# GpSimd zeroes the masked exponentials of layer two, in place of a mask added to the scores by TensorE

## The reference, cut to what matters

```python
scores = jnp.einsum('bhsl,bhtl->bhst', q_lat, c) * (1.0 / np.sqrt(L))
mask = jnp.tril(jnp.ones((Sx, Sx), dtype=bool))
scores = jnp.where(mask, scores, -jnp.inf)
w = jax.nn.softmax(scores, axis=-1)
oh = jnp.einsum('bhst,bhtd->bhsd', w, v)
```

## Time and profile before

| | us |
|---|---|
| median of 3 runs | 2285.42 (2282.18 to 2289.64) |
| the profiled execution | 2285.18 |
| its span, first to last instruction | 2283.5 |
| TensorE busy in the span | 1969.4 (86%) |
| VectorE, ScalarE, GpSimd busy | 1104.0, 864.6, 738.3 |
| mean granted TensorE clock | 0.907 of full |

### The profile page before, as it was taken

The page is one execution under the profiler, slowest core; times in us unless marked ns, Lnnn a source line. Parts: engine busy times, 40 slices in busy tenths (PEclk is TensorE's granted clock), DMA queues, the critical chain, the costliest instruction groups (busy, mean ns, idle before and its releaser), DMA issues.

```text
span 2283.5 us, 47852 instructions
## 1 busy us (share of the span) xinstructions
PE 1969.4 (86%) x16112; PEld 1298.2 (57%) x16112; DVE 1104.0 (48%) x2561; ACT 864.6 (38%) x1624; POOL 738.3 (32%) x796
## 2 busy tenths in 40 slices
PE   3464899998989999898898999998998989998978
PEld 1232475665647565565746566564756556574747
DVE  3544455462645445373645537273554536363422
ACT  2341433434343343435343343534343343533322
POOL 2000233333424333333423333342433333342425
PEclk7566899989989899999999899998999999999979
DMA  4612321313232231413231141313232141322130
GB/s 111 146 42 60 62 50 44 84 36 86 45 67 54 57 66 37 95 36 82 50 71 41 42 94 37 89 42 67 56 68 53 37 93 37 79 57 63 30 70 5
DMA packets 320767, 139.28 MB, mean 61 GB/s; under 512 B 225040, under 2 KB 306000, under 8 KB 320592
## 3 DMA queue, kind: packets, MB, share of 16 engines
q1 hardware_dynamic: 305232, 86.24, 16.0%
q0 software_dynamic: 15360, 50.34, 10.7%
HBM read 102.12 MB, written 29.88 MB: 58 GB/s over the span
## 4 chain that ended last, share of the span: by engine, by line
issue 48%; POOL 18%; PE 14%; DMA 8%; DVE 5%; SPq 3%; ACT 3%; POOLq 1%; DVEq 0%; ACTq 0%
POOL h2l L681 7%; POOL gs L675 6%; DMA cb<-comb_d 6%; PE s3r L1287 3%; POOL cb L669 3%; PE s2acc L1284 2%; POOL h1p L626 1%; SPq L539 1%; PE s2r L1287 1%; PE s2r L1495 1%; DVE th L1172 1%; SPq L500 1%; POOL va L649 1%; PE s2r L1497 1%; PE s1acc L1390 1%
## 5 line engine op out<-in xcount | busy, mean ns | idle before, releaser
L675 POOL TENSOR_TENSOR gs<-gs,cb 128x512 f32<-128x512 f32 x192 | 243.4, 1268 | 471.9 <-DVE gs L1177 285.1
L681 POOL TENSOR_TENSOR h2l<-th,h2h 128x512 f16<-128x512 f32 (+1 forms) x224 | 246.8, 1102 | 377.6 <-ACT h2h L871 377.6
L871 ACT CAST h2h<-th 128x512 f16<-128x512 f32 (+1 forms) x224 | 131.4, 587 | 499.4 <-DVE th L1172 482.1
L1287 PE MATMUL s3r<-xe,xg 128*128 128x256 f16 x2304 | 284.3, 273 | 21.1 <-issue 21.1
L1287 PE MATMUL s3r<-xe,xu 128*128 128x256 f16 x2304 | 285.0, 274 | 9.4 <-DVE th L1172 9.4
L1284 PE MATMUL s2acc<-xd,h2h 128*128 128x256 f16 x1536 | 280.3, 285 | 3.8 <-POOL h2l L681 3.5
L1177 DVE SCALAR_TENSOR_TENSOR gs<-th,s3r 128x512 f32<-128x512 f32 (+1 forms) x224 | 145.1, 648 | 266.8 <-ACT th L875 266.8
L1287 PEld LDWEIGHTS s3r<-xe,xg 128*128 128x128 f16 x2304 | 223.1, 98 | 57.5 <-issue 31.8
L1287 PEld LDWEIGHTS s3r<-xe,xu 128*128 128x128 f16 x2304 | 223.8, 98 | 42.0 <-DVE th L1172 10.0
L1172 DVE TENSOR_TENSOR th<-s3r,gs 128x512 f32<-128x512 f32 x192 | 132.6, 691 | 235.7 <-POOL gs L675 193.4
L875 ACT ACTIVATE th<-s3r 128x512 f32<-128x512 f32 (+1 forms) x224 | 126.6, 565 | 302.8 <-PE s3r L1287 302.1
(11 more groups left out here) (268 smaller groups left out, 3225.3 us busy)
## 6 DMA issues: line engine op xcount, KB each, us to landing
cb<-comb_d POOLq DMA_DIRECT2D x192, 256.0 KB, 8.0
part_d<-part SPq DMA_DIRECT2D x32, 512.0 KB, 3.3
va<-v_d SPq DMA_DIRECT2D x512, 8.0 KB
land<-part_d SPq DMA_DIRECT2D x96, 64.0 KB, 2.6
part<-part_d SPq DMA_DIRECT2D x96, 64.0 KB, 2.6
qst<-part_d SPq DMA_DIRECT2D x96, 64.0 KB, 2.3
kst<-part_d SPq DMA_DIRECT2D x96, 64.0 KB, 2.3
x<-in_L_attn_x SPq DMA_DIRECT2D x16, 256.0 KB, 2.8
```

Of the source, the lines that this page charges most:

```text
L675: g.tensor_tensor(gc2[:, p % 2, :], gs2[:, p % 2, :], cb2[:, 2 * p:2 * p + 2, :].rearrange("p a s -> p (a s)"), ALU.mult).then_inc(sem("gc ...
L681: g.tensor_tensor(h2l[0:m, n % 2, 0:w], th2[0:m, n % 2, 0:w], h2h[0:m, n % 2, 0:w], ALU.subtract).then_inc(sem("h2l_made"), 1)
L871: s.copy(h2h[0:m, n % 2, 0:w], th2[0:m, n % 2, 0:w]).then_inc(sem("h2h_made"), 1)
L1287: ins = nc.tensor.matmul(bk, lhs[i][k], rhs[j][k], start=first, stop=last)
```

## The change

The matmul of the mask (L1541) goes; the last score matmul of each head signals the bank full. GpSimd gets eight steps of its own, one per K step: it waits for both heads' exponentials and writes zeros above the diagonal into the two diagonal blocks of both slots, in one `affine_select` of 128 x 512 numbers, in place. `weigh` waits for that and no longer for the exponentials. `TURNS` is another order of the same steps.

```diff
-TURNS = [int(c) for c in ("022202121100221001210201212202102220122212101210101010131002"
-                         "021301001010310133113010004103041000040303043030033440303330"
-                         "33313")]
+TURNS = [int(c) for c in ("022221002112021010102201212202102212022212101021101013102120"
+                         "003010101101013011330310000401410300040033343300030403033343"
+                         "33130")]
@@ gp2
-            for n in range(2 * HG + 8):
+            for n in range(HG + 5):
+                yield
+            for n in range(0, H, 2):
+                for i in (n, n + 1):
+                    gp.wait_ge(*emptied2(it, U2["k_rows", i]))
+                    carry(gp, "gp_waited")
+                x = p2[:, n % PSLOT:n % PSLOT + 2, :].rearrange("p s (c n) -> p s c n", n=P)[:, :, 0:3:2, :]
+                g.affine_select(out=x, in_=x, pattern=[[0, 2], [0, 2], [1, P]], compare_op=ALU.is_ge, fill=0.0, base=0,
+                                channel_multiplier=-1).then_inc(sem("p2_masked"), 1)
+                yield
+            for n in range(3):
                 yield
@@ pe2, weigh
-                pe.wait_ge(*emptied2(it, U2["k_rows", QUAD * q + QUAD - 1]))
+                pe.wait_ge(*event("p2_masked", it, 2 * q + 2))
@@ pe2, K steps
-                        mm(ring2[u % 2][:, at:at + S - P * j], head(kst2, h, QK1)[:, P * j:P * j + P],
-                           head(qst2, h, QK1)[:, P * j:S], start=j == 0, stop=False, skip_group_check=True)
-                for u, h in pair:
-                    mm(two(ring2[u % 2])[:, :, 0:P], identb[:, :], maskk1[:, :].unsqueeze(1).to_broadcast([P, T, P]),
-                       start=False, stop=True, skip_group_check=True).then_inc(fills2(u), 1)
+                        ins = mm(ring2[u % 2][:, at:at + S - P * j], head(kst2, h, QK1)[:, P * j:P * j + P],
+                           head(qst2, h, QK1)[:, P * j:S], start=j == 0, stop=j == T - 1, skip_group_check=True)
+                        if j == T - 1:
+                            ins.then_inc(fills2(u), 1)
```

## The result

| | us |
|---|---|
| before, median of 4 runs beside those of after | 2283.8 (2280.15 to 2289.64) |
| after, median of 4 runs | 2354.33 (2338.53 to 2364.75) |
| ratio | 1.0300, 95% interval 1.0238 to 1.0363 |
| the profiled execution of after, and its span | 2355.37, 2353.7 |
| its mean granted TensorE clock | 0.894 of full (before 0.907) |

The change costs 71 us. The direction was forecast, the size was not: 2305 was predicted, and 2344 was the upper end of the range.

A forecast was written before the change was run, and what follows sets the result against it. The prediction took PE, 86% busy, as the engine to save on, its saving turned into waits. Per pass +3.1 and -1.7 give +1.4 us, +20 over 14 passes: 2285.2 + 20 = 2305 us, range 2256 to 2344.

The forecast's parts named there:

- The masks' saving: K steps: PE's time saved by dropping the masks all turns into waits for ScalarE and VectorE; weigh 3 1.7 later.
- The part ahead of T: Before the older experts' last `down` ends: two layer-one row scores move behind it, so this part loses 1.7 us.
- the sum: Per pass, +3.1 us behind the older experts' last `down`, -1.7 ahead of it: +1.4, over 14 passes +20 us.
- its sign: PE's waits at `up 3` and `k 12`: together over 3 us a pass; wrong if 2.6 or under, or K stretch shorter.
- the last stretch: Last K stretch, counted apart: masks go (5 us), four select waits of about 1 us come; put at nothing.
- one stretch of 3.4 us: PE between `k 12` and `turned 1`: half-rate clock expected after idles of 3 and 2, 1.7 us lost.
- The select: GpSimd's zeroing instruction: 0.95 us each, between 0.66 and 1.36; it hides at 0.95 and decides from about 1.3.
- The masks' worth: PE's mask matmuls in the K steps: removing them gains at most 41 us over 16 passes, at least nothing.
- A: Rival, faster: PE stays the bound, waits do not form; whole gain 2244 us, half 2265; chance 0.28.
- B: Rival, no change: K-stretch saving and the later weight transfer cancel; 2279 to 2292 us; chance 0.14.
- C: The forecast itself, slower: 2292 to 2325 us; chance 0.38.
- D: Rival, slower still: select takes 1.36 us, or PE's idle brings a further half-rate stretch; with both 2340 us; chance 0.20.

The follow-up runs named there:

- e17: The kernel after with the first 56 steps of a pass (the front) in the order of before; 2308.07 us, 1.0079 against before.
- e2: The kernel before, mask added by PE and no select, with the changed kernel's order of steps; 2361.78 us, 1.0321 against before.
- e3: The kernel after with the mask matmuls left in as well as GpSimd's zeroing; 2364.41 us, 1.0303 against before.
- e5: The kernel after with the old order of steps behind weigh 3 (the tail); 2396.09 us, 1.0459 against before.
- e9: The kernel after with the twelve weight transfers issued by SP instead of GpSimd, at the same step; 2305.67 us, 1.0092 against before.
- e14: GpSimd zeroing and weight transfers issued by SP, new order for the first 56 steps, old order behind; 2283.54 us, 0.9986 against before.
- e18: The kernel before, masks by matmul, with only the first 56 steps of a pass in the new order; 2301.25 us, 1.0076 against before.
- e1: The kernel after, with GpSimd's zeroing, but the steps in the old order; 2396.14 us, 1.0473 against before.
- e7: The kernel before with GpSimd's twelve weight transfers issued early, ahead of `xbe`; 2323.6 us, 1.016 against before.
- e8: GpSimd's zeroing in the old order, with GpSimd's twelve weight transfers issued early, ahead of `xbe`; 2345.64 us, 1.026 against before.
- e6: The kernel after with GpSimd's twelve weight transfers issued early, ahead of `xbe`; 2356.15 us, 1.0301 against before.
- e4: The kernel before without the second pass's mask, neither matmul nor select, in the old order; 2286.51 us, 0.9996 against before.
- e12: The kernel before without the second pass's mask, neither matmul nor select, old order, weight transfers issued by SP; 2253.04 us, 0.983 against before.
- e10: The kernel before, old masks and old order, with the twelve weight transfers issued by SP; 2251.7 us, 0.9823 against before.

## Why the prediction was wrong in size

**What held.** In the pass shown: weigh 0 at T + 8.3 (8.9 forecast), weigh 3 at T + 22.8 (22.7), `weights 0` at T + 23.6 (23.2), the product of `gate 2` at T + 43.0 (42.4), `up 3` at T + 45.0 (44.5), `k 12` at T + 49.8 (49.3), `turned 1` at T + 59.4 (58.0). The masks' saving is turned into waits for ScalarE: the weighs' wait for `p` went from 21.5 us to 33.9, and it is ScalarE and not the select that they wait for, as the second select was done 0.9 us before weigh 0. The part ahead of T is 2.0 us shorter (1.7 forecast). With the old front, as the prediction in effect assumed it, the sum comes out: e17's periods are 1.53 us longer than before (1.4 forecast), its T to weigh 3 1.75 (1.7), and it takes 2308 us where 2305 was forecast.

**What agreed for other reasons.** The prediction named as its sign PE's waits at `up 3` and `k 12`, together over 3 us a pass, and called itself wrong if they stay at 2.6 or under. They are 0.55 and 1.39 us in the pass shown, where idles of 3 and 2 were forecast, and 2.5 us a pass over the 14 passes, no more than before's 2.8 at `k 12` alone. By its own sign it is wrong there. `up 3` does start when the weights' chain lets it, but PE reaches it at T + 44.5 and not at T + 41.5: in the new tail it waits on the way for the next sequence's x (L960, 17.5 us in all) and for `part` (L991, 16.4), where before has 0.2 us a pass behind ScalarE and 2.6 us in all. The walk had these two at nothing. That e17 meets the sum is thus partly luck: 2.5 us a pass too much at two waits, 2.0 too little at two others, 3.3 us in all that the last stretch takes more, and 1.0 by which the first T comes sooner.

**The step that failed** is "The sum": "+3.1 behind T and -1.7 ahead of it". It took the order as changed only around the K steps. The diff also permutes the 56 steps in front (21 of their digits differ), which I neither spelled out nor walked through, and so entered as zero. On top of the new K steps and tail they cost 46 us (after against e17), mainly in three places of the table: 1.9 us a pass before the row scores (36.55 against 34.66), 1.1 from T to weigh 3, and 8.4 us at the two ends. The forecast was 49 short.

**The clock.** I gave the half rate one stretch of 3.4 us behind the idles at `up 3` and `k 12`. From weigh 3 to `turned 1` there is less of it than before, 1.5 us a pass against 2.9; it came elsewhere. Among seven kernels with the new front (after, e2, e3, e5, e9, e14, e18), 4 to 9 passes of 14 have over 3 us at half rate before the row scores, and at most one in any with the old front. (e9's profile is of its fastest execution, 2288.96 us.) Over 10 us at half rate from T to weigh 3 is found in 17 of 70 passes of the five that have the new front and the new K steps (after, e2, e3, e5, e9), in 2 of 28 of the two that have the new front and the old K steps (e14, e18), and in none with the old front, except where PE waits long within the stretch: three passes of e1, those with 12 to 14 us at weigh 3, and passes of e7 and e8, where the early weights make it wait for the row maxima (so does e6, left out of the count).

Fewer masks are not the reason (e3; and e4, without any, has 447 us at half rate in its span, before 427). From T to T the half-rate time is 13.4 us a pass in before, 16.9 in after, 10.5 in e17 and 12.6 in e18. Between e17 and after PE's idle time is nearly the same, 16.4 and 16.5 us, so the 2.7 us of the period lie in the 6.4 us more at half rate; between before and e18 idle time grows from 11.9 to 13.4 and the clock adds nothing. The front thus costs waits by itself, and clock on top of the new K steps. The tie between front and clock is shown as one that goes together; how the order in front brings the clock down in some passes and not in others stays open, and each kernel has one profile only.

**The single prices.** The select takes 0.64 us; I took 0.95 with 0.66 as the lower end, so it lies just under it. The Trainium skill's 769 ns ("GPSIMD Engine Reference", Elementwise side-by-side cycle accounting) was nearer than my value and still above the measured 637. It mattered little, since the select hides in the new order: of all the weighs of after one is put down to it, with 1.3 us. The masks' worth I bounded by 0 and 41 us; the runs say 0, to within 6 us (e4 against before; e12 against e10 agrees). The 28 us that the Trainium skill's gap of 109 ns gave ("TensorE: Matmul & The Clock Gate", Back-to-back issue gap) is PE time, and no run shows it as time of the kernel. The last stretch I put at nothing: it took 6.5 us more, 3.3 of them still in e17 (98.7 us from the last T to the end). The weights are awaited there with no tail to hide them: PE's wait for `th` of `up 3` is 13.7 us, where before has 9.2.

**The rivals.** A fell: weigh 3 isn't at T + 20.96 or before, and e4 shows that even with no select PE's saving does not reach the end. B fell by the time alone. C has the direction and the times of the landmarks, D the sign of the remainder: there was more half rate, but not behind the idle where D placed it, and its select was shorter, not longer.

**What the change is worth.** Without the new front 21 to 25 of its 71 us are left, the price of the later weights with the K steps and tail that make room for them (e17). The new front costs 46 on top of these and 14 by itself (e18), so over 30 us come only where both stand together, and no single part owns them; with SP's weights the front costs 44 on top of them and 32 by itself. Its aim, to relieve TensorE of the masks, was worth nothing here, for it relieved an engine that waits at the weighs anyway. What was to be gained lay in the issue of the weights in GpSimd's queue: moved to SP, with the old masks and the old order, the kernel takes 2251.7 us, 1.8% less than before (e10).

## What to carry to other kernels
When a diff holds a reordered list, decode and walk the whole of it, also where none of the changed operations stand; here the permutation of 56 steps cost 14 us by itself and 46 on top of the rest, which alone cost 21. Before an engine is relieved of work, leave the work out altogether and time that: it bounds the gain, and here the bound was zero. An instruction added to a queue is priced by what stands ahead of it there (in e1 weigh 3 waits 102 us for selects behind the twelve issues on GpSimd, while all selects of after take 81), and bulk transfers belong in a queue where nothing short waits behind them.

## What the hardware did that I had not expected
The twelve issues on GpSimd are sometimes cut in two by a gap without any wait, 7.82 us in e1's row above. It is regular: in all twelve kernels in which GpSimd issues them it comes behind the sixth issue of the third, eighth and thirteenth of the 16 groups, so every sixty issues, and lasts 7.8 to 9.1 us; in the eight with SP it never comes. In before these are the passes with the three longest waits at `k 12` (5.21, 4.55 and 5.15 us), in e1 those with 12 to 14 us at weigh 3. Nothing in the traces names a cause. SP needs more time for them, 9.57 us for twelve against GpSimd's 6.92, and the kernel gains all the same. A transfer of 1.7 us became one of up to 9.3 by 3 MB issued just ahead of it. And identical steps of one kernel took 22.7 us at a mean granted clock of 1.00 in one pass and 28.1 at 0.61 in the one before it, with less idle time in the longer.
